# Routed attention with an order taken from a model of the engines, three PSUM buffers for each kind of scores, and the first unit's maxima in two parts

## The chip, the cores and the metric

The kernel runs on one core of a Trainium2 chip, as one launch. The metric is the device time of the whole kernel in microseconds (us); lower is better. All data is fp32.

## What is computed

`x` is 2 sequences of 1024 tokens, 512 wide. After a layer norm (`xn`) two attentions run on the same tokens, and both are added to `x`:

```python
x = L0_attn_x
xn = _layernorm(x, axis=-1)
x = x + _L0_attn_ref(xn, ...) + _L0_ffn_ref(xn, W_gate, W_qkv)

# _L0_attn_ref: 16 heads of 32, 4 key heads, RMS norm and rotation of q and k,
# a causal window of 64 keys, softmax, output projection Wo

# _L0_ffn_ref, the "routed" attention:
gating = softmax(x @ W_gate.T)                  # 16 gates; the best one picks a head per token
k_shared = einsum('bth,bthd->btd', indicator, k)     # one key of 32 for all 16 heads
v_shared = einsum('bth,bthd->btd', gating_top1, v)   # one value of 32
att = einsum('bhqd,bkd->bhqk', q, k_shared) / sqrt(32)
att = softmax(where(causal, att, -inf))
y = einsum('bhqk,bkd->bhqd', att, v_shared)
```

The change is about the routed attention: full causal attention over 1024 keys, for 2 sequences and 16 query heads that share one key and one value per token.

## The kernel before

The program has two stages. In the first, 8 rounds of 256 tokens each make the norms, the projections (`gemm`), the windowed attention and its output projection (`project`), whose sum with `x` is stored to `partial` in DRAM. The queries of the routed attention go to `q_parts` in DRAM, its keys stay in `k_stack`, its values in `v_all`.

The second stage is the routed attention. It is cut into 8 units, numbered `u` = 2*hg + b: a group `hg` of 4 query heads (`HQ` = 4) of sequence `b`. A unit needs two passes:

- The row maxima (`row_scores`): for each block `i` of 128 queries and each head `h`, TensorE makes scores of 128 queries against their (i+1)*128 keys into `s_ps`, and VectorE adds the causal mask and takes the maximum along the row into `r_max` (one custom instruction and one that reads its accumulator). Then `row_maxima` negates and splits the maxima on VectorE, `max_in_rows` turns them on TensorE (line 846), ScalarE copies them out of PSUM, and a DMA on ScalarE's queue writes them as two more rows of the query operand `q_op`, where the second pass finds them as a bias inside its matmul.
- The weights and values: for each pair (i, j) of a query block and a key block, 36 in `PRODUCTS`, diagonal first, `key_scores` makes 128 keys by 4*128 queries into one of two banks of `st_ps`, ScalarE takes the exponential into one of 10 buffers `p_t`, GpSimd masks the diagonal blocks, and `key_values` adds the product with `v_all` to `o_ps`. There is one `o_ps`; at the end of a row ScalarE copies it out before the next row's first value product may begin, and `finish` transposes it back on TensorE and normalises it on VectorE (three operations).

Every engine runs its instructions in the order in which `make_plan` records steps, and waits on semaphores where a step's input is late. So the order of steps in the plan is the order on each engine, and a wait of one instruction holds all that stands behind it. In the second stage `phase` builds this order: it spreads the row maxima of unit u+1 evenly among the products of unit u with `merged`, by fixed weights of the steps. Value products come in groups of up to 5 (`value_groups`), three steps behind their scores (`LAG_VALUES`). PSUM holds two `s_ps` of 1024 columns (two banks each), two `st_ps`, one `o_ps` and one `tp_ps`.

Unit 0 has nothing before it. Its maxima are made by `first_maxima`, in 48 steps of at most 512 keys, which use the two PSUM rooms `gemm[1]` and `tp1` while the last two tiles of the first stage come to their end. Only when all 48 are done does `routed_banks` let the second stage begin. The queries come in by `q_load` on SP's queue: 12 DMAs for each unit (4 quarters, 3 blocks). The last tile's residual goes the way `res_load` (SP), `res_bias` (GpSimd), `project` (TensorE and VectorE), and its load may start only when the tile two before it has been stored, on SP's queue too:

```python
            elif step == "res_load":
                m, a = key
                if m:
                    lane.wait_ge(*M[f"res_stored{a}"].of(m - 1))
```

## Time and profile before

| | us |
|---|---|
| median of 3 runs | 810.26 (810.06 to 811.58) |
| the profiled execution, its own time | 807.35 |
| span of its trace | 805.9 |
| busy in the span: TensorE matmul (PE) | 710.2 (88%) |
| TensorE weight loads (PEld) | 504.0 (63%) |
| VectorE (DVE) | 516.6 (64%) |
| ScalarE (ACT) | 372.6 (46%) |
| GpSimd (POOL) | 266.2 (33%) |

The span runs from the first to the last instruction; the run's own time is 1.45 us longer. A matmul's end is modelled and matmuls overlap, so a busy PE is not a TensorE at its peak, and the distance from one start to the next says more than a duration. Names of tiles are those of the memory: `w_tok` is also the room of `q_op`, `picked_fk` that of `r_max`, `x_ln` that of the causal mask, `p_loc` and `p_loc_t` those of `p_t`, `rope_sq` and `rope_b` those of the copied rows, `k_t` that of the loaded `partial`. "PEclk" is the clock that TensorE was granted: 1.00 is 2.4 GHz, 0.50 is 1.2 GHz.

### The profile page before, as it was taken

To read this page: it belongs to the slowest core of one execution; us is meant where nothing else is said; L and a number is where in the kernel's file an instruction comes from. 1 tells how busy PE (TensorE), PEld (TensorE's weight loads), DVE (VectorE), ACT (ScalarE), POOL (GpSimd) and SP (SyncE) were. 2 spreads that over 40 slices of the span, in tenths; PEclk is the share of its full clock that TensorE was granted. 3 is DMA by queue.
4 is the path that set the end of the run, shared out by engine and by line. 5 is a ranking of instruction groups with operands and counts; after the bars stand their busy time and mean duration, and the time that the engine had idled before them with its cause. 6 is when DMAs were issued, how large, how long until landed. Compare 5 with 4: busy or idle time off the path is not lost.

```text
span 805.9 us, 13661 instructions
## 1 busy us (share of the span) xinstructions
PE 710.2 (88%) x5000; PEld 504.0 (63%) x5000; DVE 516.6 (64%) x1191; ACT 372.6 (46%) x906; POOL 266.2 (33%) x224
## 2 busy tenths in 40 slices
PE   4697999999899997998655998999899999999997
PEld 3576877788788886887522555555555555555543
DVE  4976775776758765676465675767676676757511
ACT  5354544354444644446100545545455455545464
POOL 2865653855637662774100101011010101011020
PEclk9999999999999999999955799999999999999999
DMA  8321221322112231202720103112030403110000
GB/s 301 129 89 42 70 83 57 102 63 83 48 46 82 64 96 58 70 29 70 186 82 2 40 21 95 39 54 79 22 93 21 113 20 93 40 48 27 3 27 27
DMA packets 61411, 54.67 MB, mean 68 GB/s; under 512 B 5792, under 2 KB 52256, under 8 KB 61344
## 3 DMA queue, kind: packets, MB, share of 16 engines
q1 hardware_dynamic: 59056, 52.74, 22.0%
q10 hardware_dynamic: 2288, 1.06, 0.5%
q8 instruction: 40, 0.66, 0.3%
q14 instruction: 27, 0.22, 0.1%
HBM read 35.63 MB, written 17.89 MB: 66 GB/s over the span
## 4 chain that ended last, share of the span: by engine, by line
PE 45%; ACT 4%; DVE 3%; issue 2%; DMA 2%; SPq 1%; POOL 0%; DVEq 0%; ACTq 0%
PE o_ps L872 17%; PE st_ps L858 11%; PE s_ps L835 10%; ACT p_loc L1284 2%; PE tp_ps L882 2%; PE gemm L713 2%; PE gemm L811 2%; SPq L1500 1%; ACT p_loc_t L1284 1%; DMA q_parts<-qt 1%; DVE gemm L1069 1%; PE gemm L709 1%; DMA partial<-x_res 1%; ACT p_loc L1238 0%; PE win L758 0%
## 5 line engine op out<-in xcount | busy, mean ns | idle before, releaser
L1087 DVE CUSTOM_DVE_ANT_0 s_ps<-s_ps,x_ln 128x128 f32<-128x128 f32 (+7 forms) x224 | 168.4, 772 | 85.2 <-PE s_ps L835 84.1
L713 PE MATMUL gemm<-w_tok,xt 128*128 128x512 f32 (+1 forms) x768 | 179.2, 379 | 5.0 <-DVE qt L1020 1.8
L713 PEld LDWEIGHTS gemm<-w_tok,xt 128*128 128x128 f32 x768 | 131.0, 192 | 30.1 <-DVE qt L1020 3.0
L858 PE MATMUL st_ps<-w_tok,k_stack 98*128 98x512 f32 x288 | 123.4, 460 | 20.6 <-ACT p_loc L1284 12.6
L1284 ACT ACTIVATE p_loc<-st_ps 128x512 f32<-128x512 f32 x192 | 107.3, 595 | 66.4 <-PE st_ps L858 56.6
L835 PE MATMUL s_ps<-k_stack,w_tok 96*128 96x512 f32 (+1 forms) x336 | 106.0, 380 | 7.1 <-DVE picked_fk L1087 7.0
L1403 POOL TENSOR_SCALAR_AFFINE_SELECT p_loc<-p_loc 128x512 f32<-128x512 f32 x48 | 30.1, 634 | 244.6 <-ACT p_loc L1284 244.6
L872 PE MATMUL o_ps<-p_loc,v_all 128*64 128x256 f32 x768 | 101.1, 392 | 0.0
L858 PEld LDWEIGHTS st_ps<-w_tok,k_stack 98*128 98x128 f32 x288 | 52.8, 192 | 63.7 <-ACT p_loc L1284 35.4
L835 PEld LDWEIGHTS s_ps<-k_stack,w_tok 96*128 96x128 f32 x336 | 59.3, 193 | 38.1 <-DVE picked_fk L1087 23.5
L872 PEld LDWEIGHTS o_ps<-p_loc,v_all 128*64 128x64 f32 x768 | 49.8, 137 | 36.9 <-issue 13.8
L1284 ACT ACTIVATE p_loc_t<-st_ps 128x512 f32<-128x512 f32 x96 | 55.2, 596 | 33.1 <-PE st_ps L858 30.0
L1238 ACT ACTIVATE p_loc<-win,l_max 128x96 f32<-128x96 f32 x256 | 60.9, 392 | 8.5 <-DVE l_max L1028 8.4
L1347 POOL TENSOR_TENSOR rms_y<-rms_v,minus_half 128x20 f32<-128x20 f32 x16 | 58.6, 3663 | 9.2 <-DVE rms_v L1005 9.2
L709 PE MATMUL gemm<-xt,w_qt 128*128 128x256 f32 x384 | 55.0, 288 | 6.1 <-DVE picked_fv L974 3.2
L709 PEld LDWEIGHTS gemm<-xt,w_qt 128*128 128x128 f32 x384 | 49.1, 191 | 9.6 <-DVE picked_fv L974 4.0
L799 PE MATMUL gemm<-w_o,attn_t 128*128 128x512 f32 x192 | 52.0, 406 | 1.7 <-DVE x_res L1054 1.7
L1387 POOL TENSOR_TENSOR p_loc<-p_loc,l_rec 128x1536 f32<-128x1536 f32 x16 | 44.1, 2759 | 20.8 <-DVE l_rec L1040 20.8
L872 PE MATMUL o_ps<-p_loc_t,v_all 128*64 128x256 f32 x384 | 49.5, 385 | 0.0
L1363 POOL TENSOR_TENSOR rope_b<-qkv,sin_t 128x128 f32<-128x128 f32 (+1 forms) x32 | 27.4, 879 | 64.5 <-DVE qkv L995 64.3
L1247 ACT ACTIVATE p_loc_t<-win 96x512 f32<-96x512 f32 x64 | 37.5, 605 | 22.2 <-PE win L773 22.2
L773 PE MATMUL win<-idt,p_loc 128*96 128x128 f32 x256 | 40.6, 285 | 7.4 <-ACT p_loc L1238 5.5
(114 smaller groups left out, 984.3 us busy)
## 6 DMA issues: line engine op xcount, KB each, us to landing
w_tok<-q_parts SPq DMA_DIRECT2D x96, 128.0 KB, 2.5
q_parts<-qt SPq DMA_DIRECT2D x64, 128.0 KB
x_ln<-x SPq DMA_DIRECT2D x8, 512.0 KB, 6.3
x_res<-x SPq DMA_DIRECT2D x16, 256.0 KB, 4.9
partial<-x_res SPq DMA_DIRECT2D x16, 256.0 KB, 2.0
k_t<-partial SPq DMA_DIRECT2D x8, 512.0 KB, 5.9
raw<-w_tok SPq DMA_DIRECT2D x3, 1024.0 KB, 13.0
v_win<-v_rows SPq DMA_DIRECT2D x64, 48.0 KB, 2.7
```

Source lines behind the costliest of these rows:

```text
L709: i = e.matmul(g[:, 0:PAIR], w_qt_p[r][:, k, a * P:(a + 1) * P], xs[l][:, k, :], start=first, stop=last)
L713: i = e.matmul(g[:, 0:cols], xs[l][:, k, a * P:(a + 1) * P], w_tok_p[r][:, k, c0:c0 + cols], start=first, stop=last)
L773: i = e.transpose(win[0:KEYS, quad, g * P:(g + 1) * P], p_loc[a][:, g, quad, :], idt[:, :])
L799: i = e.matmul(gemm[bank][:, :], attn_t[l][:, kc, :], w_o_p[r][:, kc, :], start=kc == 0 and q == 0, stop=kc == KC - 1 and q == 2)
L835: mm = e.matmul(s_ps[n][:, c0:c0 + cols], q_op[b][0:HALVES, h, i * P:(i + 1) * P], k_stack[0:HALVES, b * S + c0:b * S + c0 + cols], start= ...
L858: e.matmul(st_ps[k % 2][:, :, :], k_stack[0:HALVES + 2, b * S + j * P:b * S + (j + 1) * P], q_op[b][0:HALVES + 2, :, i * P:(i + 1) * P], s ...
L872: mm = e.matmul(o_ps[c * VW:(c + 1) * VW, :, :], v_all[:, b * IT + j, :], p_t[k % RING][:, 2 * c:2 * c + 2, :], start=i == j, stop=ends_ro ...
L1087: e.tensor_tensor_reduce(out=s[:, 0:width], in0=s[:, 0:width], in1=causal[:, S - width:S], scale=1.0, scalar=NEG, op0=ALU.add, op1=ALU.max ...
L1238: i = e.activation(p_loc[a][:, g, quad, :], win[:, g, quad * KEYS:(quad + 1) * KEYS], ACT.Exp, bias=l_max[:, a, n:n + 1])
L1284: e.activation(p_t[k % RING][:, :, :], st_ps[k % 2][:, :, :], ACT.Exp, scale=ROUTED_SCALE).then_inc(*M["rp_exp"].did((u, k)))
L1347: e.tensor_tensor(rms_y[:, :], rms_v[:, :], minus_half[:, :].to_broadcast([P, NH]), ALU.pow).then_inc(*M["rms_r"].did((n, a)))
L1387: e.tensor_tensor(p_l, p_l, l_rec[:, a, :].unsqueeze(2).to_broadcast([P, H, KEYS]), ALU.mult).then_inc(*M["p_r"].did((m, a)))
```

## The change

- `make_plan` loses `phase`, `merged` and `weights_and_values`. A class `Routed` takes their place: it keeps a clock and the time at which each engine and each buffer comes free, by fixed costs, and at each point records the step that its model can start first, of four kinds: finish a row, scores of keys, a step of the row maxima, a group of values.
- Row maxima are made in pieces of at most 512 keys (`MAXIMA`, 48 steps in a unit where there were 32; the blocks 4 to 7 have two pieces for a head, whose maxima meet in one more operation, `r_far`). There are three `s_ps` of one bank where there were two of two banks, and three `st_ps` where there were two.
- Unit 0: `first_maxima` makes only the blocks 0 to 3 (`PART` = 4; 16 steps, none with a second piece) once the first stage's products are all placed. They are turned and written to `q_op` as part 0, with 4 DMAs, one for a head. The other 32 steps stand in the second stage, as part 1 with 4 more DMAs, and the products of rows 4 to 7 of unit 0 wait for it.
- The last round makes `fv` ahead of `qt`, and the queries of sequence 0 are loaded right after `fv`, those of sequence 1 after the last `qt` as before.
- `max_in_rows` goes through `s_ps[0]`, where it went through `tp_ps`.

```diff
-LAST_UNITS = [("kvg", 0), ("q", 0), ("fk", 0), ("kvg", 1), ("q", 1), ("fk", 1), ("qt", 0), ("qt", 1), ("fv", 0),
-              ("fv", 1), ("qt", 2), ("qt", 3)]
+LAST_UNITS = [("kvg", 0), ("q", 0), ("fk", 0), ("kvg", 1), ("q", 1), ("fk", 1), ("fv", 0), ("fv", 1), ("qt", 0),
+              ("qt", 1), ("qt", 2), ("qt", 3)]
...
+MAXIMA = [(i, h, c0) for i in range(IT) for h in range(HQ) for c0 in range(0, (i + 1) * P, 512)]
+S_BANKS, ST_BANKS = 3, 3
...
+        if (n, kind, a) == (ROUNDS - 1, "fv", 1):
+            do("routed_rooms")
+            for quarter in range(4):
+                do("q_load", 0, 0, 0, quarter)
...
         if (n, kind, c) == (ROUNDS - 1, *LAST_UNIT):
-            do("routed_rooms")
-            for b in range(B):
-                for quarter in range(4):
-                    do("q_load", b, 0, b, quarter)
+            for quarter in range(4):
+                do("q_load", 1, 0, 1, quarter)
...
         for i in range(IT):
+            if i >= PART and p.alone or i == IT - 1:
+                break
...
+            if i == PART - 1:
+                do("row_maxima", 0, 0, 0)
+                yield 0, [("V", 0.6)]
+                p.take("tp1", ("max_in_rows", 0, 0, 0), ("r_t", (0, 0)))
+                do("max_in_rows", 0, 0, 0)
...
+    def next_maximum(self):
+        if not self.maxima:
+            return None
+        u, t = self.maxima[0]
+        if t == len(MAXIMA):
+            return max(self.maxima_ready, self.s_free[0])
+        q = self.q_ready.get((u, MAXIMA[t][0] // 2))
+        return q if q is None else max(q, self.s_free[t % S_BANKS])
...
+    def next_scores(self):
+        if self.scored == UNITS_ROUTED * len(PRODUCTS):
+            return None
+        u, k = divmod(self.scored, len(PRODUCTS))
+        whats = [self.row_ready.get((u, int(u == 0 and k >= row_start(PART)))), self.st_free[k % ST_BANKS]]
...
+    def run(self):
+        rows = UNITS_ROUTED * IT
+        while self.finished < rows:
+            ways = [(self.next_finish(), self.take_finish), (self.next_scores(), self.take_scores),
+                    (self.next_maximum(), self.take_maximum), (self.next_values(), self.take_values)]
+            ways = [(max(ready + ROOM, self.now), n, take) for n, (ready, take) in enumerate(ways)
+                    if ready is not None]
+            start, _, take = min(ways)
+            self.now = start
+            take()
...
-    s_ps = [pb(top, f"s_ps{n}", [P, S]) for n in range(2)]
-    st_ps = [pb(top, f"st_ps{n}", [P, HQ, P]) for n in range(2)]
+    s_ps = [pb(top, f"s_ps{n}", [P, 512]) for n in range(S_BANKS)]
+    st_ps = [pb(top, f"st_ps{n}", [P, HQ, P]) for n in range(ST_BANKS)]
...
             elif step == "key_scores":
                 u, b, k = key
                 i, j = PRODUCTS[k]
                 if k == 0:
-                    lane.wait_ge(*M["r_row"].of(u))
-                if k >= 2:
-                    lane.wait_ge(*M["rp_exp"].of((u, k - 2)))
+                    lane.wait_ge(*M["r_row"].of((u, 0)))
+                if (u, k) == (0, row_start(PART)):
+                    lane.wait_ge(*M["r_row"].of((0, 1)))
+                if k >= ST_BANKS:
+                    lane.wait_ge(*M["rp_exp"].of((u, k - ST_BANKS)))
...
+                for h in range(HQ) if u == 0 else ():
+                    e.dma_start(q_op[b][HALVES:HALVES + 2, h, i0 * P:(i0 + count) * P].bitcast(F32),
+                                in_rows[2 * h * count:2 * (h + 1) * count, :].bitcast(F32)).then_inc(
+                                    *M["r_row"].did((u, part), inc=16))
```

Where instructions move. First SP's queue at the end of the first stage: `q_parts<-qt` are the last stores of the queries, `w_tok<-q_parts` the `q_load` of the first two units, `partial<-x_res` and `x_res<-x` the store and the load of the residual. Before:

```order
L1441 DMA q_parts<-qt 4x32x256 x2
L1479 DMA v_win<-v_rows 96x128 x4
L1441 DMA q_parts<-qt 4x32x256 x4
L1500 DMA w_tok<-q_parts 32x4x256 x24
L1485 DMA partial<-x_res 128x512
L1452 DMA x_res<-x 128x512
L1485 DMA partial<-x_res 128x512 x2
```

Now:

```order
L1550 DMA q_parts<-qt 4x32x256 x4
L1613 DMA w_tok<-q_parts 32x4x256 x12
L1550 DMA q_parts<-qt 4x32x256 x4
L1594 DMA partial<-x_res 128x512
L1561 DMA x_res<-x 128x512
L1613 DMA w_tok<-q_parts 32x4x256 x12
L1594 DMA partial<-x_res 128x512 x2
```

The 24 query loads that stood in one piece ahead of the residual's store and load are now 12 ahead of the last query stores and 12 behind the residual's store and load.

Next TensorE in the middle of a unit, at the row of 5 products (`o_ps` x10; two matmuls stand for one product): `s_ps` is a step of the row maxima, `st_ps` one of the scores of keys, `tp_ps<-idt,rope` a finish. Before:

```order
L872 MATMUL o_ps<-p_loc,v_all 64x256 x10
L835 MATMUL s_ps<-k_stack,w_tok 128x512
L835 MATMUL s_ps<-k_stack,w_tok 128x256
L835 MATMUL s_ps<-k_stack,w_tok 128x512
L835 MATMUL s_ps<-k_stack,w_tok 128x256
L858 MATMUL st_ps<-w_tok,k_stack 128x512 x4
L835 MATMUL s_ps<-k_stack,w_tok 128x512
L835 MATMUL s_ps<-k_stack,w_tok 128x384
L872 MATMUL o_ps<-p_loc,v_all 64x256 x2
L872 MATMUL o_ps<-p_loc_t,v_all 64x256 x6
L835 MATMUL s_ps<-k_stack,w_tok 128x512
```

Now:

```order
L968 MATMUL o_ps<-p_loc,v_all 64x256 x10
L954 MATMUL st_ps<-w_tok,k_stack 128x512 x3
L978 MATMUL tp_ps<-idt,rope_sq 128x128 x2
L926 MATMUL s_ps<-k_stack,w_tok 128x256
L926 MATMUL s_ps<-k_stack,w_tok 128x512
L954 MATMUL st_ps<-w_tok,k_stack 128x512
L926 MATMUL s_ps<-k_stack,w_tok 128x256
L968 MATMUL o_ps<-p_loc,v_all 64x256 x2
L968 MATMUL o_ps<-p_loc_t,v_all 64x256 x6
L954 MATMUL st_ps<-w_tok,k_stack 128x512 x3
L926 MATMUL s_ps<-k_stack,w_tok 128x512
L926 MATMUL s_ps<-k_stack,w_tok 128x256
```

Between the group of 5 products and the next stood 6 matmuls of row maxima before, and 3 now; the scores of keys stood four together with two banks to hold them, and come three and one with three banks.

Last TensorE at the seam of two units: `picked_fk` is `max_in_rows` of the next unit, the last groups of `o_ps` are the values of row 7. Before:

```order
L858 MATMUL st_ps<-w_tok,k_stack 128x512 x3
L846 MATMUL tp_ps<-idt,picked_fk 64x128
L858 MATMUL st_ps<-w_tok,k_stack 128x512
L872 MATMUL o_ps<-p_loc_t,v_all 64x256 x4
L872 MATMUL o_ps<-p_loc,v_all 64x256 x4
L882 MATMUL tp_ps<-idt,rope_sq 128x128 x2
L858 MATMUL st_ps<-w_tok,k_stack 128x512
L835 MATMUL s_ps<-k_stack,w_tok 128x256 x3
L872 MATMUL o_ps<-p_loc,v_all 64x256 x8
L835 MATMUL s_ps<-k_stack,w_tok 128x256 x3
```

Now:

```order
L926 MATMUL s_ps<-k_stack,w_tok 128x384
L968 MATMUL o_ps<-p_loc_t,v_all 64x256 x4
L968 MATMUL o_ps<-p_loc,v_all 64x256 x4
L926 MATMUL s_ps<-k_stack,w_tok 128x512 x3
L968 MATMUL o_ps<-p_loc,v_all 64x256 x8
L926 MATMUL s_ps<-k_stack,w_tok 128x512 x3
L978 MATMUL tp_ps<-idt,rope_b 128x128 x2
L926 MATMUL s_ps<-k_stack,w_tok 128x512 x2
L939 MATMUL s_ps<-idt,picked_fk 64x128
L926 MATMUL s_ps<-k_stack,w_tok 128x256 x8
L926 MATMUL s_ps<-k_stack,w_tok 128x384
```

Before, `max_in_rows` stood ahead of the last 8 value products of its neighbour, with scores of the next unit prepared. Now 8 steps of the maxima (512 keys each) stand between or behind the last value products, `max_in_rows` behind them all, and then 9 short steps of the maxima of the unit after next, before the first scores of keys of the next unit.

## Rows read from the trace of the kernel before

**Rows 1.** Windows: busy us (instructions) of each engine, granted clock, DMA share.

```profile
400.00:420.00 20.00, 10.12 (x20) 4.98 (x19) 10.84 (x37) 0.00 (x0) 1.26 (x1) 0.63 0.31 92
420.00:440.00 20.00, 12.26 (x21) 5.45 (x20) 13.56 (x43) 0.27 (x1) 0.00 (x0) 0.50 0.00 0
600.00:640.00 40.00, 37.16 (x217) 21.92 (x217) 26.11 (x77) 20.51 (x41) 4.39 (x7) 1.00 0.21 57
```

**Rows 2.** Line 846, the turned maxima: the seven later ones, and unit 0's.

```profile
L846 PE MATMUL tp_ps<-idt,picked_fk x7: 269/270/272, 486.0 to 758.8; 128*64 128x128 f32 x7
...
438.42 0.39 PE L846 MATMUL tp<-idt,picked_fk 128*64 128x128 f32 x1 [1.70 <-DVE picked_fk L1101]
```

**Rows 3.** Timeline, end of the first stage: residual of the last tiles.

```profile
383.29 0.63 DVE L1054 TENSOR_TENSOR x_res<-gemm,x_res 128x512 f32<-128x512 f32 x1
...
384.79 6.17 SPq L1500 DMA_DIRECT2D w_tok<-q_parts  x12
...
396.70 0.43 SPq L1485 DMA_DIRECT2D partial<-x_res  x1
...
399.56 0.86 PE L799 MATMUL gemm<-w_o,attn_t 128*128 128x512 f32 x3
...
401.02 0.35 SPq L1452 DMA_DIRECT2D x_res<-x  x1
...
403.92 1.26 POOL L1380 TENSOR_TENSOR x_res<-x_res,bias_o 128x512 f32<-128x512 f32 x1 [17.71 <-DMA x_res<-x]
405.28 0.69 DVE L1054 TENSOR_TENSOR x_res<-gemm,x_res 128x512 f32<-128x512 f32 x1 [4.79 <-POOL x_res L1380]
```

**Rows 4.** Timeline, from unit 0's turned maxima to its first scores.

```profile
439.15 1.15 ACTq L1268 DMA_DIRECT2D w_tok<-w_tok  x1
442.24 0.29 PEld L858 LDWEIGHTS st_ps<-w_tok,k_stack 98*128 98x128 f32 x1 [3.73 <-issue]
```

**Rows 5.** Windows: one whole unit in the middle.

```profile
601.70:647.20 45.50, 42.20 (x248) 24.96 (x247) 30.49 (x91) 23.32 (x46) 5.03 (x8) 1.00 0.21 59
```

**Rows 6.** Timeline of PE and ACT, a row of five value products and after.

```profile
601.68 2.38 PE L872 MATMUL o_ps<-p_loc,v_all 128*64 128x256 f32 x20
603.99 0.96 PE L835 MATMUL s_ps<-k_stack,w_tok 96*128 96x512 f32 x4
604.79 0.63 PE L858 MATMUL st_ps<-w_tok,k_stack 98*128 98x512 f32 x2
...
605.23 1.09 ACT L1284 ACTIVATE p_loc_t<-st_ps 128x512 f32<-128x512 f32 x2 [0.73 <-PE st_ps L858]
...
605.88 0.98 PE L858 MATMUL st_ps<-w_tok,k_stack 98*128 98x512 f32 x2 [0.45 <-ACT p_loc_t L1284]
```

**Rows 7.** Groups by line and form, second stage: count, busy us, mean ns.

```profile
L1087 DVE CUSTOM_DVE_ANT_0 s_ps<-s_ps,x_ln 128x512 f32<-128x512 f32 x24 | 16.4, 706 | 4.8 <-PE s_ps L835 4.3
L1087 DVE CUSTOM_DVE_ANT_0 s_ps<-s_ps,x_ln 128x128 f32<-128x128 f32 x24 | 6.8, 306 | 13.0 <-PE s_ps L835 13.0
L1087 DVE DVE_READ_ACCUMULATOR2_ANT picked_fk<- 128x1 f32 x201 | 28.4, 141 | 0.0
L1108 DVE RECIPROCAL picked_fk<-tp_ps 128x4 f32<-128x4 f32 x60 | 10.7, 179 | 53.3 <-PE tp_ps L882 53.3
L1118 DVE TENSOR_TENSOR x_res<-picked_fv,k_t 128x128 f32<-128x128 f32 x32 | 10.2, 319 | 1.1
```

**Rows 8.** Timeline of DVE, two steps of 512 keys in a row.

```profile
458.16 0.69 DVE L1087 CUSTOM_DVE_ANT_0 s_ps<-s_ps,x_ln 128x512 f32<-128x512 f32 x1
...
458.77 0.73 DVE L1087 CUSTOM_DVE_ANT_0 s_ps<-s_ps,x_ln 128x512 f32<-128x512 f32 x1
```

**Rows 9.** Windows around the clock's rise, columns as in rows 1.

```profile
450.00:452.00 2.00, 2.00 (x7) 1.15 (x6) 0.39 (x1) 0.46 (x2) 0.00 (x0) 0.50 0.00 0
...
454.00:456.00 2.00, 2.00 (x15) 1.23 (x14) 1.22 (x6) 0.41 (x2) 0.00 (x0) 1.00 0.04 8
```

**Rows 10.** Timeline, the last unit: its last transposes.

```profile
801.24 0.44 PE L882 MATMUL tp_ps<-idt,rope_b 128*128 128x128 f32 x2 [0.48 <-ACT rope_b L1295]
```

More of the change, by code:

```diff
@@ L370, in first_maxima @@
     def first_maxima():
[L371 to L373 removed]
+        while p.fk_stacked < ROUNDS - 1 or bank_free[1] is None or bank_free[1] > p.now:
             yield None
@@ L386, in first_maxima @@
                         yield None
-                    p.busy(p.now, ("V", 0.2 + cols / 960))
+                    p.busy(p.now, ("V", 0.4 + cols / 960))
                     t += 1
-        do("first_far", t - 1)
-        do("row_maxima", 0, 0)
-        yield 0, [("V", 0.6)]
-        p.take("tp1", ("max_in_rows", 0, 0), ("r_t", 0))
-        do("max_in_rows", 0, 0)
-    value_groups, group = {}, []
-    for k in range(len(PRODUCTS)):
-        group.append(k)
-        if ends_row(k) or len(group) == VALUES_AT_ONCE and not ends_row(k + 1):
-            value_groups[k], group = group, []
@@ L492, with routed_stage @@
+def routed_stage(p):
+    Routed(p).run()
 class Mark:
@@ L642, in mixed_attention_kernel @@
     r_max_t = w_rooms[0].piece(P, rows=2 * HQ * IT)
+    r_first_t = [w_rooms[0].piece(P, rows=2 * HQ * PART) for _ in range(2)]
     causal = Room(x_ln).piece(S)
@@ L647, in mixed_attention_kernel @@
     r_max_p = small.piece(2, HQ, IT)
+    r_first_p = [small.piece(HQ, 2, PART).rearrange("p h s i -> p s h i") for _ in range(2)]
     o_rec = small.piece(2, 2)
```

320 lines of the change are left out of this document (189 added, 131 removed).

## The prediction

> **What bounds the kernel now.** I read the windows first. In the second stage TensorE has work in nearly every microsecond [rows 1, 5], but between 400 and 440 us it is half idle, VectorE is busy some 60% and ScalarE not at all [rows 1]: there `first_maxima` alone makes the maxima of unit 0, with two PSUM rooms, and TensorE is granted 0.50, its 1.2 GHz, for all of 420 to 440. The turned maxima mark the units: unit 0's pass line 846 at 438.42, unit 1's at 486.0, unit 7's at 758.8 [rows 2]. So a unit in the middle takes (758.8 - 486.0)/6 = 45.47 us, the first 47.6, and what follows the last mark 805.9 - 758.8 = 47.1.
>
> The timeline of the end of the first stage shows what holds the last tile. The residual of one tile is ready at 383.29 + 0.63 = 383.9, but its store is issued at 396.70, since SP is busy from 384.79 with 24 query loads (12 of them took 6.17 us). The load that waits for it goes at 401.02, GpSimd adds the bias at 403.92, and VectorE has the last residual at 405.28 + 0.69 = 406.0 [rows 3]. Before, this cost less than its length, because the maxima had to run to 437 anyway, though behind it.
>
> In one middle unit of 45.50 us TensorE is busy 42.20, VectorE 30.49, ScalarE 23.32 [rows 5]. Busy overstates TensorE, so I take its needs from starts: 5 value products in 603.99 - 601.68 = 2.31, that is 0.46 each; four matmuls of maxima in 604.79 - 603.99 = 0.80, 0.20 to 0.22 each; scores of keys about 0.24 each (two are charged 0.63 with the pipeline's end) [rows 6]. A unit then needs 36 x 0.46 + 36 x 0.24 + 48 x 0.22 = 35.8, plus 8 finishes of two short transposes, which I put at 0.15 to 0.2 each: 37 us. The other 8 are waits: with two `st_ps` the third scores start at 605.88, 0.10 after the first exponential (605.23 + 0.55, half of the two rows' 1.09) [rows 6].
>
> **The change, part by part**, as a walk from mark to mark, made against the span.
>
> *Start.* Only 16 of 48 steps remain ahead of the stage, and they stand between the last tile's transposes and projections. By the new SP order the residual's store follows 383.9 at once. Store to load took 401.02 - 396.70 = 4.3 and load to bias 2.9, bias 1.3 [rows 3], so the last residual has its bias at 384 + 4.3 + 2.9 + 1.3 = 392.5, well ahead of its projection. That projection, not the DMA, then ends the first stage; in the trace its last part runs at 399.56 + 0.86 = 400.4 [rows 3], with maxima between its parts, as now. With the last steps of maxima, the residual on VectorE (0.69) and two small operations I put the first mark at 403, against 438.4: **-35.4**. Bounds: 400 (nothing behind the projection) and 411 (the residual path stays as late as 406.0, and 16 steps' rest behind it).
>
> *Unit 0* then has more in it. From mark to first scores took 442.24 - 438.42 = 3.8, with one DMA of which the issue took 1.15 [rows 2, 4]. Now ScalarE issues four; at a half to the whole of 1.15 each the first scores are 5.5 to 7.5 behind the mark, say 6, and since three steps of maxima fill the three banks ahead of them, VectorE idles most of that. Behind it 29 steps of part 1 remain. A step of 512 keys costs VectorE 0.61 from start to start to 0.71 alone [rows 7, 8], I take 0.65; one of 128 costs 0.31, of which (512 - 128 keys at (0.706 - 0.306)/384 = 1.04 ns) 0.17 is fixed. 15 x 0.65 + 4 x 0.26 + 4 x 0.38 + 4 x 0.52 + 4 x 0.65, less two, is 16 us; four finishes of three operations, 0.18, 0.32 and a middle one that I put at 0.29, 0.79 each [rows 7], 3.2; the closing operations 0.8. TensorE's part is 10 x 0.46 + 10 x 0.24 + 29 x 0.22 = 13.4 at 2.4 GHz, but it starts at 1.2 GHz. In the trace the clock came back between 452 and 454, ten us after the first scores at 442.24, with TensorE busy all the time [rows 4, 9]; in such ten us it does 5 us of its work, and VectorE falls 3 behind. 6 + 16 + 3.2 + 0.8 + 3 = 29 from mark to part 1's mark.
>
> Then 5.2 to the scores of row 4 (3.8 and three more issues at about 0.5); 4.5 until eight scores have passed ScalarE at 0.55 (half of 1.09, [rows 6]) and row 4's values may start; 21 to the end of row 7's values (as in the middle units below); and behind these VectorE still has 4 steps of 384 keys and 11 of 512 (4 x 0.52 + 11 x 0.65 = 9.2, for the order puts 15 of the 32 there), a finish 0.8 and the closing 0.8: 10.8. Sum 41.5. Unit 0: 29 + 41.5 = 70.5 against 47.6: **+22.9**. Bounds 62 (full clock, issues 0.5) and 77 (half clock throughout part 1).
>
> *Six middle units.* By the new order of TensorE, from a mark: 3.6 to the first scores (the wait for the written maxima, covered by 9 short steps). To row 3's values: 16 scores x 0.24, 13 maxima x 0.22, 6 products x 0.46, 3 finishes: 10.0, and 0.8 of waits for exponentials, since ScalarE has 13 exponentials and three copies in it. From there to row 7's first group: 22 products 10.1, 20 scores 4.8, 18 maxima 4.0, finishes 0.8, waits 0.7: 20.4. There TensorE is full and VectorE is not: per group of four or five products (1.9 to 2.3 us) it gets three steps, of 0.65, 0.3 and 0.65. So the maxima fall behind, and the seam pays: 8 products 3.7 and three matmuls 0.7, then VectorE's last 5 steps of 512 (3.3), a finish 0.8, the closing operations and their hops 1.2: 9.7. Sum 3.6 + 10.8 + 20.4 + 9.7 = 44.5 against 45.47. The three `st_ps` thus take the exponentials' waits out of the middle, and the seam gives most of it back. VectorE's own total, 30.5 [rows 5] and 16 more fixed parts of 0.17 (2.7), is 33.2, below both. Six times -1.0: **-5.8**. Bounds per unit 40 (TensorE's 37 and the seam's wait of 3) and 48 (the walk's error, two extra hops in each of ten group changes).
>
> *Last unit.* Nothing but products: its mark to scores 3.6; then by the same walk without maxima 29.6, as ScalarE's 36 x 0.55 and the rows' copies now run under the values; from the last transposes to the end 805.9 - 801.24 = 4.7 as before [rows 10]. 37.9 against 47.1: **-9.2**. Bounds 35 and 42.
>
> Sum: 805.9 - 35.4 + 22.9 - 5.8 - 9.2 = 778.4 of span, and 1.45 for what lies around it: 779.9. The profiled execution, 807.35, was 2.9 below the median of the runs; ratios carry over better than differences, so between 779.9 and 810.26 x 779.9/807.35 = 782.7 I say **781**.
>
> A wait moved: `max_in_rows` now shares `s_ps[0]` with the maxima, so the next unit's first step waits for ScalarE's copy, about 0.7, inside the 3.6 above; for units 1 to 7 TensorE has nothing else queued there but these short steps. The moved query loads (12 behind the residual load) are needed only by unit 1, at 430. `r_far`, one operation of 0.2 per unit, is in the closing operations.
>
> **Rivals.**
> - *The middle keeps up* (0.16). If TensorE's steps are shorter than I took, or the waits at group changes vanish, VectorE is fed and the seam shrinks to the DMA's 3: units of 41 us, 781 - 6 x 3.5 = 760. For it: VectorE has 11 idle us in a unit. Against it: the order is fixed, with three steps per group.
> - *The start stays late or unit 0 runs at half clock* (0.15): +7 from either bound, 788 to 796. For it: TensorE at 0.50 from 420 on [rows 1]; against it, part 1 gives TensorE scores and products that `first_maxima` didn't have.
> - *The clock falls at every seam; slower at the end* (0.11, of which 0.04 slower than before). In the trace the clock is 1.00 through all middle units, where the matmuls are spread evenly [rows 5], and 0.50 where TensorE had about half of its time [rows 1]. Now each seam, from row 7's last values to the first scores, is some 9 us in which TensorE has 3 of work, and rows 0 to 2 follow. Half clock costs what TensorE would have needed: 3 to 4 for a seam alone (hidden in part, 781 + 7 x 3 = 802), 11 if it lasts through rows 0 to 2 (781 + 7 x 9 = 844). It decides from 29/7 = 4.1 us lost per seam. I hold the long form unlikely, as TensorE is full again all through rows 0 to 2. The Trainium skill, "TensorE: Matmul & The Clock Gate", on a second failure mode, says that cycling through PSUM banks can let TensorE idle in small gaps often enough that its clock swings; by that page these seams would be such a place, and its outcome is this rival's.
> - *The order does nothing* (0.05): units stay at 45.5 or go to 47 and the gain of the start is eaten by unit 0: 795 to 806.
> - The forecast itself has 0.53 (its own range 770 to 791).
>
> **Numbers.** A measurement of this kernel can tell about 0.2%, 1.6 us. Faster needs less than 808.6: all but the long clock case and the worst of the others, 0.94; within 0.2% 0.01; slower 0.05. The range 758 to 800 leaves out the fastest of the first rival (0.05) and the clock and the do-nothing cases above 800 (0.12).
>
> **What would show it.** Line 846's successor has nine marks: the first near 403 (401 to 407), part 1's near 432, unit 1's near 473, then every 44.5, the last near 740. If the last residual is still at 406, the SP step is wrong. In a middle unit VectorE's steps of row 7 should run back to back after the last values with TensorE idle, and the windows of the seam should still show 1.00; 0.50 there would prove the clock rival. ScalarE's waits for scores in the last unit should be nearly gone. A distance of marks below 42 or above 47 makes the prediction wrong by its largest term.

## The result: slower, and where the time went

The changed kernel took **829.76 us** (median of 4 runs, 826.92 to 830.24) beside 810.16 for the kernel before (807.65 to 811.58): a ratio of **1.0238**, 95% interval 1.0203 to 1.0273. The prediction said 781 with a range of 758 to 800 and gave "slower" 0.05. It was wrong, and by far more than its range.

The page of the profile after shows it at once in the row of TensorE's clock, which in the slices of the second stage no longer reads 9:

```profile
span 829.0 us, 14064 instructions
...
PE   4797999999799989996688989799897989979787
...
PEclk9999999999999999998886959879697896969979
```

Line 939 is what line 846 was [rows 2]. It has nine marks, as the prediction said: one on `tp` at 408.51, then 440.18, 483.34, 533.55, 584.62, 633.96, 684.74, 735.02 and 785.95 on `s_ps`. First and last are in its groups:

```profile
L939 PE MATMUL s_ps<-idt,picked_fk x8: 272/392/394, 440.2 to 785.9; 128*64 128x128 f32 x7, 128*32 128x128 f32 x1
...
L939 PE MATMUL tp<-idt,picked_fk x1: 269/269/269, 408.5 to 408.5; 128*32 128x128 f32 x1
```

Set against the prediction's sum, on the span (829.0 against 778.4, so 50.6 too little):

| term | predicted | measured | off by |
|---|---|---|---|
| first mark | 403 | 408.51 | +5.5 |
| unit 0 (two marks) | 29 + 41.5 = 70.5 | 31.7 + 43.2 = 74.8 | +4.3 |
| a middle unit, (785.95 - 483.34)/6 | 44.5 | 50.44 | +5.9, six times 35.6 |
| behind the last mark | 37.9 | 43.05 | +5.2 |

Seven tenths of the miss are the middle units. Windows of whole units, columns as in [rows 1], show busy times and clock; first the fifth of the six middle units, then what lies behind the last mark:

```profile
684.74:735.02 50.28, 46.22 (x246) 29.00 (x246) 32.94 (x123) 22.36 (x45) 5.04 (x8) 0.84 0.18 52
...
785.95:829.00 43.05, 34.67 (x197) 19.16 (x197) 6.60 (x24) 22.08 (x45) 5.03 (x8) 0.86 0.06 18
```

Against [rows 5] TensorE is busy 4 us longer with the same work, and the clock is 0.84 in place of 1.00. Finer windows, across one seam and what follows, show when:

```profile
529.00:531.00 2.00, 1.16 (x4) 0.37 (x2) 1.97 (x8) 0.00 (x0) 0.00 (x0) 1.00 0.00 0
531.00:533.00 2.00, 0.00 (x0) 0.00 (x0) 1.83 (x8) 0.00 (x0) 0.00 (x0) 0.69 0.29 89
533.00:535.00 2.00, 1.00 (x4) 0.77 (x4) 0.37 (x2) 0.27 (x1) 0.00 (x0) 0.50 0.92 238
...
545.00:547.00 2.00, 2.00 (x7) 1.64 (x6) 1.38 (x6) 1.01 (x3) 0.63 (x1) 0.50 0.00 0
547.00:549.00 2.00, 2.00 (x10) 0.77 (x8) 1.35 (x5) 1.03 (x2) 0.00 (x0) 0.54 0.13 43
549.00:551.00 2.00, 2.00 (x14) 1.35 (x12) 0.53 (x3) 1.66 (x4) 0.55 (x1) 1.00 0.48 154
```

From 531 to 533 VectorE makes the last maxima and TensorE has nothing at all; the clock falls there to 0.50, 1.2 GHz, and stays there until 548, though TensorE is wholly busy from 539 on. That is the rival that the prediction named and held unlikely. Its own test, "0.50 there would prove the clock rival", is met in all of the seams; the six middle units have a mean clock of 0.83 to 0.88.

The timeline of TensorE across that seam has the wait itself:

```profile
526.09 1.95 PE L968 MATMUL o_ps<-p_loc,v_all 128*64 128x256 f32 x16
...
529.43 1.15 PE L926 MATMUL s_ps<-k_stack,w_tok 96*128 96x512 f32 x2 [0.28 <-DVE picked_fk L1179]
533.55 0.39 PE L939 MATMUL s_ps<-idt,picked_fk 128*64 128x128 f32 x1 [2.96 <-DVE picked_fk L1204]
...
538.57 1.65 PE L954 MATMUL st_ps<-w_tok,k_stack 98*128 98x512 f32 x3
```

The start has a stall that the prediction didn't see. At the end of the first stage the kernel after shows:

```profile
377.46 2.24 SPq L1550 DMA_DIRECT2D q_parts<-qt  x4
...
382.71 0.38 ACT L1309 ACTIVATE qt<-gemm 128x256 fp32r<-128x256 f32 x1 [6.50 <-DMA q_parts<-qt]
383.12 0.42 DVE L1116 TENSOR_TENSOR qt<-gemm,qt 128x256 fp32r<-128x256 f32 x1 [5.36 <-ACT qt L1309]
...
383.60 1.65 PE L891 MATMUL gemm<-w_o,attn_t 128*128 128x512 f32 x3 [6.15 <-DVE qt L1116]
...
390.24 0.69 DVE L1150 TENSOR_TENSOR x_res<-gemm,x_res 128x512 f32<-128x512 f32 x1 [0.76 <-PE gemm L891]
390.95 1.16 SPq L1594 DMA_DIRECT2D partial<-x_res  x1
...
397.89 0.36 SPq L1561 DMA_DIRECT2D x_res<-x  x1
...
400.91 1.26 POOL L1489 TENSOR_TENSOR x_res<-x_res,bias_o 128x512 f32<-128x512 f32 x1 [8.59 <-DMA x_res<-x]
...
402.05 0.68 DVE L1150 TENSOR_TENSOR x_res<-gemm,x_res 128x512 f32<-128x512 f32 x1
...
405.67 0.86 PE L891 MATMUL gemm<-w_o,attn_t 128*128 128x512 f32 x3
...
406.59 0.69 DVE L1150 TENSOR_TENSOR x_res<-gemm,x_res 128x512 f32<-128x512 f32 x1
...
408.51 0.27 PE L939 MATMUL tp<-idt,picked_fk 128*32 128x128 f32 x1 [1.75 <-DVE picked_fk L1204]
```

The products `qt` now stand last, close behind each other. ScalarE's copy of one waits 6.5 us until the stores of an earlier one have read its room, and TensorE's projection waits for the bank behind it. So the residual that was ready at 383.9 [rows 3] now comes at 390.9; its store does follow at once, as the prediction had it, but from a later point. The last residual, at 406.59, has waited for the last part of its projection (405.67 + 0.86 = 406.5); its bias was there at 400.91 + 1.26 = 402.2.

### The profile page after: what moved, and what is told of

Same layout as the page of the kernel before. It is cut to its first block, busy times and chain, and to the rows that moved or that the text cites. A ratio compares the mean times of both kernels' runs of the same rounds, so it can differ in the third digit from the quotient of the medians.

```text
span 829.0 us, 14064 instructions
## 1 busy us (share of the span) xinstructions
PE 731.1 (88%) x5001; PEld 531.0 (64%) x5001; DVE 532.0 (64%) x1424; ACT 365.3 (44%) x907; POOL 265.7 (32%) x224
## 4 chain that ended last, share of the span: by engine, by line
PE 46%; DVE 6%; DMA 3%; issue 2%; ACT 1%; ACTq 0%; SPq 0%; DVEq 0%
PE o_ps L968 17%; PE st_ps L954 12%; PE s_ps L926 9%; DVE s_ps L1179 3%; DMA w_tok<-w_tok 2%; PE tp_ps L978 2%; PE gemm L805 2%; PE gemm L891 1%; DVE picked_fk L1179 1%; PE win L865 1%; DVE qkv L1109 1%; DMA q_parts<-qt 1%; PE av L877 1%; PE win L850 0%; PE s_ps L939 0%
## 5 line engine op out<-in xcount | busy, mean ns | idle before, releaser
L1179 DVE CUSTOM_DVE_ANT_0 s_ps<-s_ps,x_ln 128x512 f32<-128x512 f32 (+2 forms) x368 | 197.6, 586 | 67.1 <-PE s_ps L926 66.2
L926 PE MATMUL s_ps<-k_stack,w_tok 96*128 96x512 f32 (+2 forms) x368 | 134.8, 458 | 10.5 <-DVE picked_fk L1179 5.3
L1393 ACT ACTIVATE p_loc<-st_ps 128x512 f32<-128x512 f32 x192 | 103.0, 599 | 81.3 <-PE st_ps L954 80.3
L954 PE MATMUL st_ps<-w_tok,k_stack 98*128 98x512 f32 x288 | 115.2, 491 | 9.3 <-DMA w_tok<-w_tok 9.2
L968 PE MATMUL o_ps<-p_loc,v_all 128*64 128x256 f32 x768 | 106.0, 406 | 0.0
L926 PEld LDWEIGHTS s_ps<-k_stack,w_tok 96*128 96x128 f32 x368 | 77.1, 232 | 42.5 <-DVE picked_fk L1179 25.6
L954 PEld LDWEIGHTS st_ps<-w_tok,k_stack 98*128 98x128 f32 x288 | 58.7, 226 | 49.7 <-issue 20.2
L1211 DVE RECIPROCAL picked_fk<-tp_ps 128x4 f32<-128x4 f32 x64 | 11.6, 181 | 88.2 <-PE tp_ps L978 88.2
L801 PEld LDWEIGHTS gemm<-xt,w_qt 128*128 128x128 f32 x384 | 49.2, 191 | 10.9 <-DVE picked_fv L1070 5.8
L1393 ACT ACTIVATE p_loc_t<-st_ps 128x512 f32<-128x512 f32 x96 | 51.9, 600 | 9.2 <-PE st_ps L954 8.7
L1179 DVE DVE_READ_ACCUMULATOR2_ANT picked_fk<- 128x1 f32 x368 | 51.8, 141 | 0.0
```

Source lines behind the costliest of these rows:

```text
L801: i = e.matmul(g[:, 0:PAIR], w_qt_p[r][:, k, a * P:(a + 1) * P], xs[l][:, k, :], start=first, stop=last)
L926: e.matmul(s_ps[t % S_BANKS][:, 0:cols], q_op[b][0:HALVES, h, i * P:(i + 1) * P], k_stack[0:HALVES, b * S + c0:b * S + c0 + cols], start=T ...
L954: e.matmul(st_ps[k % ST_BANKS][:, :, :], k_stack[0:HALVES + 2, b * S + j * P:b * S + (j + 1) * P], q_op[b][0:HALVES + 2, :, i * P:(i + 1) ...
L968: mm = e.matmul(o_ps[c * VW:(c + 1) * VW, :, :], v_all[:, b * IT + j, :], p_t[k % RING][:, 2 * c:2 * c + 2, :], start=i == j, stop=ends_ro ...
L1179: e.tensor_tensor_reduce(out=s[:, 0:cols], in0=s[:, 0:cols], in1=causal[:, S - width + c0:S - width + c0 + cols], scale=1.0, scalar=NEG, o ...
L1393: e.activation(p_t[k % RING][:, :, :], st_ps[k % ST_BANKS][:, :, :], ACT.Exp, scale=ROUTED_SCALE).then_inc(*M["rp_exp"].did((u, k)))
```

## The experiments

All ratios are to the kernel before on the same chip, with 95% intervals. "Unit" is the distance of two marks in the middle.

### Is it the clock? Fill the seams, or put a seam where none was

**a_fill.** The changed kernel, in every seam matmuls that write `o_ps` and are thrown away; nothing is left out. A pair is four such matmuls in the trace.

```diff
+            elif step == "filler":
+                for _ in range(key[0]):
+                    for c in range(2):
+                        e.matmul(o_ps[c * VW:(c + 1) * VW, :, :], v_all[:, c, :], v_all[:, 0:4, :],
+                                 start=True, stop=True)
```

> The changed kernel with idle TensorE time at every seam filled by matmuls whose result is thrown away (they write o_ps between the last row's copy and the next unit's first value product): 2 pairs behind the last values, 1 behind each of the next maxima steps, 6 behind the last one, 1 behind max_in_rows, 4 ahead of the next scores. Theory C (the seam leaves TensorE idle, the clock drops to 0.50 there and stays so for some 15 us into the next unit): the granted clock stays at 1.00 in the second stage from unit 1 on, marks come every 44 to 46 us instead of 50.4, the time falls to 785 to 800. Rival W (the 50 us units come of waits in the order itself, the clock is only a companion): the clock rises, but the marks stay at 49 to 52 and the time at 825 to 835, since the fillers add work and take none away.

834.68 us, 1.0298 (1.0274 to 1.0323). The clock was 1.00 in four of six middle units, but these took 48.3 to 48.6, between what the two theories expected: 16 fillers ahead of the first scores put them 6.1 us behind the mark (546.14 to 552.24), where the changed kernel has 5.0. The kernel's time lies in rival W's range of 825 to 835. But a filler that lies on the path itself tells nothing clean, so a lighter one followed.

**e_fill2.** The same with fewer.

```diff
-FILLERS = {"behind values": 2, "between": 1, "behind last": 6, "behind rows": 1, "ahead of scores": 4}
+FILLERS = {"behind values": 1, "between": 1, "behind last": 4, "behind rows": 1, "ahead of scores": 0}
```

> The changed kernel with a lighter set of the discarded matmuls: 4 rows behind a unit's last values, 4 between its last maxima, 16 behind the last of them, 4 behind the turning, and none ahead of the first scores (a_fill had 8, 4, 24, 4 and 16), so that they stand only where TensorE was idle. Theory (TensorE at 1.2 GHz through rows 0 to 2 of every unit costs some 6 us a unit): the granted clock stays at 1.00 in most of each unit, the units take 44 to 47 instead of 50.3 and the kernel takes 790 to 808. Rival (the order itself makes the unit long, and the clock only follows idle time): the clock rises but the units stay at 48 to 50, 820 to 832. If the clock still falls behind the turning, the run doesn't tell the two apart, and the time is 822 to 832.

830.14 us, 1.0241 (1.0209 to 1.0273). The clock held in one middle unit and fell in the five others, and for that case the expectation said that the time doesn't tell the two apart. It is also blurred by unit 0, which has two seams and more fillers in them (some 100 matmuls more than in the changed kernel, a middle unit some 30): its two windows take 38.0 + 48.0 = 86.0 where the changed kernel's take 74.8, and that takes back most of the 6 x (50.4 - 48.3) = 13 us which the middle gained.

```profile
411.04:448.99 37.95, 32.52 (x156) 17.27 (x156) 22.66 (x79) 7.34 (x15) 2.49 (x4) 0.78 0.18 53
448.99:497.00 48.01, 46.25 (x226) 26.18 (x224) 29.76 (x111) 15.60 (x31) 2.54 (x4) 0.82 0.14 40
```

What tells them apart are the middle units beside each other, for they have the same instructions in the same order and differ in the clock. Windows from mark to mark:

```profile
497.00:542.44 45.44, 44.45 (x276) 27.07 (x274) 33.12 (x123) 22.04 (x45) 5.03 (x8) 1.00 0.14 43
542.44:590.05 47.61, 45.95 (x274) 27.89 (x274) 33.36 (x123) 22.15 (x45) 5.03 (x8) 0.96 0.19 57
...
637.72:687.11 49.39, 47.47 (x274) 28.70 (x274) 32.76 (x123) 22.36 (x45) 5.03 (x8) 0.93 0.20 57
687.11:737.44 50.33, 48.86 (x273) 29.77 (x274) 32.77 (x123) 22.36 (x45) 5.03 (x8) 0.90 0.18 52
```

Full clock 45.4, and the longer the clock is down, the longer the unit. A mean of 0.90 over 50.3 us is 2 x 0.10 x 50.3 = 10 us at 1.2 GHz, and it costs 50.3 - 45.4 = 4.9: half of it. The same step by step, the unit at 1.00 beside the one of the changed kernel at 533.55 (0.83):

| from | to | prediction's walk | e_fill2, 1.00 | after |
|---|---|---|---|---|
| mark | first scores | 3.6 | 3.8 | 5.0 |
| first scores | row 3's values | 10.8 | 10.9 | 15.3 |
| row 3's values | row 7's first group | 20.4 | 20.5 | 20.5 |
| row 7's first group | next mark | 9.7 | 10.2 | 10.2 |
| sum | | 44.5 | 45.4 | 51.1 |

So the walk was right within 1 us at 2.4 GHz. All of the rest, 1.2 and 4.4, lies where the clock is down.

**c_even and f_seam.** c_even keeps the change's buffers, pieces, start and two parts, but merges maxima and products evenly, as before; f_seam is c_even with the last two maxima, `row_maxima` and `max_in_rows` (the 4 steps of `HELD`) behind the last row; the planned pause behind the turning (`way`) goes with it.

```diff
 c_even -> f_seam
+HELD = 4
...
-        run(main, ahead)
-        ahead = maxima(u + 1) if u + 1 < UNITS_ROUTED else []
-        run(tail, ahead[:HEAD_MAXIMA])
+        run(main, ahead[:-HELD])
+        run(tail)
+        run(ahead[-HELD:])
+        ahead = maxima(u + 1, way=False) if u + 1 < UNITS_ROUTED else []
+        run(ahead[:HEAD_MAXIMA])
```

> The changed kernel (three s_ps and three st_ps, steps of 512 keys, unit 0 in two parts, new start) with the old rule for the order: the maxima of unit u+1 spread evenly over the products of unit u, instead of the model's order. Theory C: no seam without TensorE work, so the clock stays at 1.00 from unit 1 on, and units take 40 to 44 us; the time is 760 to 785. Rival B (banks and pieces are what costs: 16 more VectorE steps and shorter matmuls): units stay at 48 us or more whatever the order, 815 or more.

> c_even with a seam put in: the last two maxima of every unit and their turning stand behind the last values and the last row of the unit before, and the rest keeps the even merging. c_even has units of 44.8 and a clock of 1.00 in them. Theory (a seam costs its idle time, some 3 to 5 us, and then a stretch at 1.2 GHz that costs some 6 more): the clock shows 0.50 for more than 10 us in every middle unit, units of 52 to 56, the kernel 848 to 875. Rival (a seam costs its idle time alone): the clock stays near 1.00 and the units take 47 to 49, the kernel 815 to 828.

c_even: 799.18 us, 0.9869 (0.9849 to 0.9889), units of 44.8 at 1.00. That is faster than both kernels, but outside the 760 to 785 that I had expected. f_seam: 839.63 us, 1.0364 (1.033 to 1.0398). One unit of each, and of f_seam the fall:

```profile
619.80:664.59 44.79, 41.38 (x246) 25.00 (x246) 32.05 (x123) 22.45 (x46) 5.14 (x8) 1.00 0.23 60
```

```profile
589.70:640.66 50.96, 46.89 (x246) 27.91 (x246) 32.99 (x123) 22.59 (x45) 5.08 (x8) 0.87 0.18 53
...
587.00:591.00 4.00, 0.97 (x5) 0.71 (x4) 2.34 (x9) 0.27 (x1) 0.00 (x0) 0.85 0.60 157
591.00:595.00 4.00, 3.51 (x9) 2.26 (x9) 3.48 (x18) 0.00 (x0) 0.00 (x0) 0.50 0.43 114
...
603.00:607.00 4.00, 4.00 (x25) 2.51 (x24) 2.70 (x10) 2.44 (x5) 0.63 (x1) 0.94 0.01 4
```

A seam alone adds 6.2 us to a unit. TensorE is busy 46.89 - 41.38 = 5.5 longer with the same matmuls, and idle 0.7 longer (50.96 - 46.89 against 44.79 - 41.38). The theory's 52 to 56 were too high and the rival's 47 to 49 too low, but what is added is slower work and not waiting: the mechanism is the clock, its price about 5.5.

### Is the model's order good without its seam?

**g_lead.** One line of the planner: where both could start, a maximum goes ahead of scores.

```diff
-            ways = [(self.next_finish(), self.take_finish), (self.next_scores(), self.take_scores),
-                    (self.next_maximum(), self.take_maximum), (self.next_values(), self.take_values)]
+            ways = [(self.next_finish(), self.take_finish), (self.next_maximum(), self.take_maximum),
+                    (self.next_scores(), self.take_scores), (self.next_values(), self.take_values)]
```

> The changed kernel with one line of its planner turned: where a maximum and the first scores could both start, the maximum goes first. In its order 28 of the 36 products' values, not all 36, stand ahead of the turning from the second on, so eight products are left to cover it. Theory (the seam with its fall of the clock is what makes the units 50.3, not the model's order as such): the clock stays at 1.00 from the third unit on, units of 43.5 to 45.5, the kernel 778 to 798. Rival (an order by the model is slower than the even merging for other reasons, its short groups or its waits): units of 46 to 50, the kernel 805 to 830.

**769.97 us, 0.9506** (0.9481 to 0.953), below the range that I gave. The first of the six middle units takes 42.3 at 0.84, the other five 40.2 in the mean at 1.00, with TensorE idle for only 0.15 us in the one shown:

```profile
608.42:648.38 39.96, 39.81 (x245) 24.83 (x246) 32.24 (x123) 22.40 (x46) 5.13 (x8) 1.00 0.26 67
```

In its timeline the turning stands between values, with 8 products still to come, and waits 0.15 us where the changed kernel's waited 2.96:

```profile
607.54 0.73 PE L954 MATMUL st_ps<-w_tok,k_stack 98*128 98x512 f32 x2
608.42 0.27 PE L939 MATMUL s_ps<-idt,picked_fk 128*64 128x128 f32 x1 [0.15 <-DVE picked_fk L1204]
608.55 0.41 PE L978 MATMUL tp_ps<-idt,rope_sq 128*128 128x128 f32 x2
608.89 1.08 PE L968 MATMUL o_ps<-p_loc_t,v_all 128*64 128x256 f32 x8
```

The changed kernel's 50.4 thus divide: 40.2 of work, 5.2 that the seam costs at full clock (45.4 in e_fill2, what its fillers cost by themselves included), and 5.0 by the clock that the seam brings down.

**k_banks2, p_s2, q_st2.** g_lead in the very same order of steps, with two buffers for both kinds, for the maxima, for the scores.

```diff
-S_BANKS, ST_BANKS = 3, 3
+S_BANKS, ST_BANKS, PLANNED_BANKS = 2, 2, 3   # k_banks2; p_s2: 2, 3, 3; q_st2: 3, 2, 3
```

> g_lead with the very same order of steps, but two buffers in place of three for the maxima and two in place of three for the scores. Theory (in this order TensorE never waits because a third buffer stands ready): units of 42 to 45 in place of 40.2, a clock of 1.00 still, the kernel 782 to 808. Rival (the order alone makes the units short, the third buffers are worth nothing): units under 41, the kernel 769 to 776.

> g_lead in the very same order, with two buffers in place of three for the maxima alone. k_banks2, with two of both kinds, took 879.2 and units of 55. Theory (VectorE's passes of 0.6 us with a product of TensorE between them need two buffers in hand, so this is the kind that costs): units of 48 to 54, the kernel 825 to 870. Rival (it is the scores' buffers, which follow each other in runs of three): units under 43, the kernel 770 to 792.

> g_lead in the very same order, with two buffers in place of three for the scores alone. Theory (the maxima's buffers are those that cost): units of 41 to 44, the kernel 775 to 800. Rival (the scores stand in runs of three in this order, so the third waits for ScalarE's exponential of the first, some 0.9 us each time): units of 46 to 54, the kernel 815 to 870.

k_banks2 879.21 us, 1.0879 (1.0853 to 1.0905), units of 52 to 57; p_s2 854.29, 1.0544 (1.0514 to 1.0574), units of 50 to 54; q_st2 797.32, 0.9845 (0.9819 to 0.987). One unit of k_banks2, one of p_s2, one of q_st2, all at 1.00:

```profile
721.30:773.05 51.75, 44.37 (x246) 24.70 (x245) 34.17 (x123) 23.21 (x46) 5.08 (x8) 1.00 0.20 52
```

```profile
653.31:703.92 50.61, 43.13 (x247) 24.96 (x246) 34.19 (x123) 22.76 (x46) 5.07 (x8) 1.00 0.20 53
```

```profile
621.42:664.52 43.10, 41.72 (x246) 24.93 (x245) 32.52 (x123) 23.30 (x46) 5.14 (x8) 1.00 0.25 63
```

In this order and at full clock the third buffer of the maxima is worth 50.6 - 40.2 = 10.4 us a unit. That of the scores is worth 2.9 in the unit shown and up to 3.8 in others. For k_banks2 both of my ranges were too low, and the clock didn't stay at 1.00 as I had expected: its only middle unit at 1.00 takes 51.75, the others 55 to 57 at 0.83 to 0.97, so part of its loss is the clock's again. An order made for three buffers is far worse with two than the old order was. c_even, where three buffers stand under the old rule for the order (and the maxima come in more and shorter pieces), gains only 0.7 a unit. Order and buffers have to be counted together.

### The start and the first unit

**b_sp.** The kernel before with the new order of the last products and loads alone.

```diff
-LAST_UNITS = [..., ("fk", 1), ("qt", 0), ("qt", 1), ("fv", 0),
-              ("fv", 1), ("qt", 2), ("qt", 3)]
+LAST_UNITS = [..., ("fk", 1), ("fv", 0), ("fv", 1), ("qt", 0),
+              ("qt", 1), ("qt", 2), ("qt", 3)]
```

> The kernel before with one part of the change: fv ahead of qt in the last round and the first 12 query loads right behind fv, the other 12 behind the residual's load. Theory: the residual's 12 us on SP were partly paid for, since VectorE stood 4.8 us ahead of the last residual with maxima queued behind it; with the new order the mark of unit 0 comes 3 to 6 us earlier and the time is 804 to 808. Rival: VectorE was bound by its 48 steps anyway or the first stage gets longer by the moved loads: mark and time within 1.5 us of before.

813.62 us, 1.0052 (1.0031 to 1.0073): slower by half a per cent, with the mark at 442.21, 3.8 later than the 438.42 of [rows 2]. Neither the theory nor the rival had that. Its waits show the stall of the changed kernel, so the stall comes from this order:

```profile
PE gemm L801 <- DVE qt L1022: 5.8, 1, 5.8
```

**d_onepart.** The changed kernel with all 48 maxima of unit 0 ahead of its scores.

```diff
-            if i >= PART and p.alone or i == IT - 1:
-                break
```

The turning of part 0 stays where it was; the first scores wait for both parts.

> The changed kernel with all 48 maxima steps of unit 0 ahead of the second stage, as before the change (part 1 is then turned and written at once, and the first scores wait for both). Theory: the split alone is worth the difference of the two starts: first scores at 440 to 444 instead of 415.5, but the walk from there to unit 1's mark 45 to 48 instead of 68; the time is 5 to 10 us above the changed kernel's, 834 to 842. Rival: the split gains nothing, because unit 0's clock and waits ate it: within 3 us of the changed kernel.

836.6 us, 1.0311 (1.0283 to 1.034). In the changed kernel the two parts are worth 6.8 us by the medians and some 6 by the ratios, as expected.

**i_oldlast, j_lead_old.** c_even and g_lead with the old order of the last products and loads (b_sp's diff backwards).

> c_even (799.2) with the old order of the last units of the first stage, the tokens' rooms and the first loads of the queries behind the last product again, as before. Theory (the new order of the first stage costs a stall of TensorE near 385 and some 4 us, as in b_sp, and gives back about as much by the earlier first part): 796 to 803. Rival A (the earlier start is worth the 8 us or more by which the first turning comes ahead of a late one): 806 to 812. Rival B (the new order of the first stage is a loss here too): 790 to 796.

> g_lead (770.0) with the old order of the last units of the first stage, as i_oldlast had it over c_even (797.2 against 799.2). Theory (the new first stage gives back by its earlier first part no more than the stall near 385 costs it): 764 to 771. Rival (with the shorter units the earlier start shows in full): 775 to 780.

797.17 us, 0.9818 (0.9783 to 0.9853), and 769.61, 0.9514 (0.9492 to 0.9536). The intervals overlap those of c_even (just) and g_lead: with two parts the new first stage is worth nothing that these runs can tell. i_oldlast met its theory; j_lead_old did too.

**m_lead_one, o_one_new.** g_lead with one part (d_onepart's edit), with the old and with the new first stage.

> g_lead with the old end of the first stage and the first unit's maxima in one part, so that of the change only the model's order (maxima first), the pieces of 512 keys and the buffers are left. The first turning then falls near 438 as before, the second 44 to 47 later, then 40.2 a unit. Theory (the earlier start and the two parts are worth little once the units are short): 762 to 775. Rival (the two parts are worth the 7 us that d_onepart lost): 774 to 784.

> g_lead with the new order of the first stage, and the first unit's maxima in one part. Theory (the two parts are what costs 6 us, by a seam of their own at half clock in the first unit; the order of the first stage is worth nothing either way): 761 to 766, as m_lead_one (763.3). Rival (the new first stage costs, and the parts cost little): 767 to 772.

763.27 us, 0.9438 (0.9421 to 0.9455), and **759.92 us, 0.9384** (0.936 to 0.9408), the best of all and a little under what I had expected. With one part the new first stage is worth 3.4 us, where I had expected nothing. And here the two parts *cost* 6 and 10 us. Without them unit 0 has one seam where it had two. o_one_new's windows from mark to mark; the first holds the rest of unit 0's maxima, the second unit 0's products:

```profile
409.67:437.54 27.87, 17.55 (x34) 8.53 (x34) 19.32 (x64) 0.27 (x1) 0.00 (x0) 0.56 0.15 43
437.54:479.81 42.27, 39.91 (x209) 25.45 (x210) 31.33 (x117) 20.98 (x42) 5.08 (x8) 0.84 0.10 29
479.81:519.99 40.18, 40.03 (x248) 25.02 (x247) 32.32 (x123) 23.23 (x47) 5.14 (x8) 1.00 0.27 67
```

The next unit's mark is at 479.81 where g_lead has 485.40, and the one after at 519.99 against 527.71: 7.7 of the 8.3 us between the two spans are there by then.

**n_lead_fill.** g_lead with e_fill2's filler in its two first seams alone.

```diff
-            seam = step[1] < UNITS_ROUTED - 1
+            seam = step[1] < 1
```

> g_lead with the light filler of e_fill2 in its two first seams alone (unit 0's second part and unit 1's maxima), where g_lead still shows a clock of 0.50 for some 14 and some 13 us. Theory (that half clock costs TensorE's work there twice its time): 760 to 767, with a clock over 0.95 between the second and the fourth turning. Rival (the stretches are paced by VectorE's maxima and not by TensorE): 768 to 774.

771.02 us, 0.9529 (0.9501 to 0.9556): the rival's figure, but the clock of over 0.95 that the theory asked for wasn't reached, so the run doesn't decide. The clock rose only from 0.87 to 0.88 and from 0.84 to 0.92 in the two units. The second mark came 2.3 us later (447.35), unit 0's second part took 42.2 where g_lead had 40.4, and only the unit behind it was shorter, 40.3 for 42.3. So the fillers cost what they bring; how much of unit 0 is the clock's and how much VectorE's stays open.

## Why the prediction was wrong, step by step

*What bounds it now* held: before, the middle was at 1.00 and TensorE full.

*Start (403).* 408.5, within the bounds of 400 to 411, but for a cause that was not in the text. "The residual's store follows 383.9 at once" failed: the moved `qt` products hold TensorE for 6.15 us and the residual comes at 390.9. What ends the first stage is the last projection, as the step had it, but at 406.5 and not at 400.4: 6.1 later, about the length of that stall. So the last residual is no earlier than before (406.59 for 405.28), the sign that was to mean "the SP step is wrong", though it no longer waits for the DMA: the bias came at 402.2, 9.7 later than the 392.5 of the step, and still ahead of the projection. The step counted the DMAs that were moved out of the residual's way and not what the reordered products wait for on ScalarE. That the mark stayed within the bounds is partly luck.

*Unit 0 (70.5).* 74.8, within 62 to 77. From mark to scores it was 415.45 - 408.51 = 6.9 for 6, with the four DMAs issued in 3.22 where I had put 2.3 to 4.6:

```profile
409.11 3.22 ACTq L1373 DMA_DIRECT2D w_tok<-w_tok  x4
...
415.45 0.80 PE L954 MATMUL st_ps<-w_tok,k_stack 98*128 98x512 f32 x1 [4.86 <-DMA w_tok<-w_tok]
```

TensorE had more to do than before, as the step said, and the clock came back near 419, but it fell again near 433, ahead of the second mark; the step had one fall. The window that answers to one of [rows 1]:

```profile
420.00:440.00 20.00, 16.95 (x74) 9.04 (x73) 17.89 (x65) 3.95 (x9) 0.64 (x1) 0.82 0.07 21
```

*Six middle units (44.5).* **This is the step that failed.** Every part of the walk holds at 2.4 GHz (45.4 in e_fill2's unit at 1.00), and the bounds of 40 and 48 were bounds on the walk alone. The walk put a seam of 9.7 us in each unit, with TensorE waiting, and then let TensorE go on at full clock. The rival "the clock falls at every seam" had the true place and the true sign: in its long form I gave 844 and little more than nothing, "as TensorE is full again all through rows 0 to 2". The trace shows TensorE full there and the clock at 0.50 all the same, for some 9 us of full work (539 to 548). The evidence was in the trace of before: there too the clock stayed at 0.50 for ten us after the first scores with TensorE full [rows 4, 9], and I used that for unit 0 and not for the other seams. As to the price, 9 us a unit in the long form was too much: it measured 5 to 6. The 9 us of full work at 1.2 GHz cost the 4.4 of the table, half of their length, and the rest of the stretch (532 to 539 of 532 to 548) lies in the seam, where TensorE waits for others anyway, and costs 1.2.

The Trainium skill, "TensorE: Matmul & The Clock Gate", in its section "HAM oscillation — how this bites in real kernels", describes just this form: a wait between blocks of work, and every block starting with the slow clock. The trace agrees, with 1.00 to 0.50 at every seam. The page prices the penalty at the throttled time times 1 - 1.2/2.4; for the 17 us at 0.50 in a unit (2 x 0.17 x 51.07) by that page it would cost an estimated 8.7. If only the time in which TensorE works counts as throttled, 13.66 us here, the estimate by the page is 6.8:

```profile
532.00:548.00 16.00, 13.66 (x35) 8.75 (x37) 9.70 (x40) 5.80 (x12) 2.49 (x4) 0.50 0.33 94
```

Measured it is 51.07 - 45.44 = 5.6, for the reason above. The prediction weighed the page's other failure mode, small gaps in cycling through banks. A seam is one long wait and not that, and no run here shows that mode: c_even and g_lead cycle through three banks at 1.00.

*Last unit (37.9).* 43.05, outside 35 to 42. It is the same step: 785.95 to 798.00 are at 0.50. The first scores start 4.1 behind the mark for 3.6, and from there to 798 TensorE works without a pause at 1.2 GHz, 8 us that would be 4 at 2.4 GHz. That makes some 4.5 of the 5.2; the rest is the walk's. From the last transposes to the end it was 829.0 - 824.38 = 4.6, as predicted [rows 10]:

```profile
790.04 2.76 PE L954 MATMUL st_ps<-w_tok,k_stack 98*128 98x512 f32 x5 [3.70 <-DMA w_tok<-w_tok]
...
824.38 0.44 PE L978 MATMUL tp_ps<-idt,rope_b 128*128 128x128 f32 x2 [0.48 <-ACT rope_b L1404]
```

g_lead's 40.1 behind its last mark can't be set beside it, since eight value products of the unit before lie in them.

*Rivals.* "The middle keeps up" gave 41 a unit and 760 in all, and asked that the waits at group changes vanish. It is not what happened, but one line of the planner makes such a middle: 40.2 at 1.00. That the kernel without the two parts then took 759.9 is luck as far as the 760 goes, for its start and first unit are others than those that the 760 was added up from. "The start stays late" and "the order does nothing" are not what happened. In the chances the fault was one of size: the clock rival needed 4.1 us lost per seam for a slower kernel, it lost 5.0 in the mean (50.4 - 45.4) beside the other misses, and it had 0.04.

What stays open: which part of the two parts' cost in g_lead is clock and which is a second round of the turning and its DMAs; and why the clock fell in some of e_fill2's units and not in others that have the same instructions.
